# Which beats of the coupling take the score-maximum units: units by twos and fours alone

## The reference, cut to what matters

```python
x = x + layernorm(attn(layernorm(x)))     # 16 heads of width 8 on the left 128 columns
x = x + layernorm(ffn(layernorm(x)))

def attn(x):
    q, k, v = (left @ W.T for W in (Wq, Wk, Wv))          # per head
    att = softmax(einsum('qhd,khd->qkh', q, k) / 4, axis=k)
    return einsum('qkh,khd->qhd', att, v) @ Wo.T + bo

def ffn(x):                                # 3 cycles
    gf = global_net(x.mean(rows))
    for _ in range(3):
        tf = sigmoid(w4(gelu(w3(gelu(w2(gelu(w1(x))))))))
        coupling = 0.1 + ar * (0.7 * gf + 0.3 * tf - 0.5) * 2
        x = x + coupling * twist(x)
```

## Time and profile before

| | |
|---|---|
| median of 3 runs | 3399.24 us |
| span of the profiled execution | 3391.6 us |
| median less span | 7.6 us |
| PE busy | 3222.9 us (95%) |
| DVE busy | 2992.7 us (88%) |
| ACT busy | 2843.6 us (84%) |
| POOL busy | 897.6 us (26%) |
| mean granted TensorE clock | 0.985 |
| chain that ended last | PE 67%, DVE 17%, ACT 8%, issue 3%, SP queue 2% |
| unit's reduction, DVE line 966 (ring banks) | x3744, 683 ns each |
| unit's matmul, PE line 481 (ring banks) | x3744, 384 ns each |

### The profile page before, as it was taken

How to read it: one execution, slowest core, us unless ns; L and a number is a source line. 1 busy time by engine, 2 the same in 40 slices (tenths; PEclk the granted TensorE clock), 3 DMA queues, 4 the chain that set the end, 5 groups by cost and what they waited for, 6 DMA issues and landing times.

```text
span 3391.6 us, 56526 instructions
## 1 busy us (share of the span) xinstructions
PE 3222.9 (95%) x19712; PEld 941.5 (28%) x19712; DVE 2992.7 (88%) x5577; ACT 2843.6 (84%) x3752; POOL 897.6 (26%) x1322
## 2 busy tenths in 40 slices
PE   6989999999999999999999999999999999999987
PEld 2222232322323232232322323232232322323223
DVE  7999989999898998989989898998989989898943
ACT  3868979798897979979798897979979798896975
POOL 5002050321505123050320505123050320504015
PEclk7998999999999999999999999999999999999999
DMA  3111111121111112121121111112121121111001
GB/s 90 26 41 43 32 50 33 44 50 44 50 31 51 43 39 55 33 61 32 44 49 44 50 31 51 42 39 55 33 61 32 45 49 44 38 32 51 8 22 38
DMA packets 97498, 144.75 MB, mean 43 GB/s; under 512 B 49472, under 2 KB 60096, under 8 KB 89408
## 3 DMA queue, kind: packets, MB, share of 16 engines
q1 hardware_dynamic: 93520, 123.83, 13.8%
q0 software_dynamic: 3696, 17.31, 2.8%
HBM read 34.61 MB, written 32.51 MB: 20 GB/s over the span
## 4 chain that ended last, share of the span: by engine, by line
PE 67%; DVE 17%; ACT 8%; issue 3%; SPq 2%; DMA 1%; POOL 1%; DVEq 0%; POOLq 0%; ACTq 0%
PE heads_ps L514 24%; PE ring_ps L481 15%; DVE max_parts L966 12%; PE scoresT_ps L499 11%; PE scoresT_ps L602 7%; ACT p_sb L719 4%; DVE stats L977 3%; PE scoresT_ps L607 2%; ACT headsT L728 1%; PE ring_ps L543 1%; SPq L346 1%; DVE state L1030 1%; ACT state L784 1%; DVE moments L987 1%; PE ring_ps L529 1%
## 5 line engine op out<-in xcount | busy, mean ns | idle before, releaser
L966 DVE TENSOR_REDUCE max_parts<-ring_ps 128x1 f32<-128x512 f32 x3744 | 2369.2, 683 | 225.4 <-PE ring_ps L481 166.3
L719 ACT ACTIVATE p_sb<-scoresT_ps 128x1024 f32<-128x1024 f32 x2048 | 1970.1, 1024 | 81.4 <-PE scoresT_ps L499 57.7
L481 PE MATMUL ring_ps<-k_rows,q_rows 48*128 48x512 bf16 x3744 | 1086.0, 384 | 33.1 <-DVE max_parts L966 23.8
L514 PE MATMUL heads_ps<-p_sb,v_sb 128*9 128x512 f32 x8192 | 1071.4, 595 | 17.9 <-ACT headsT L728 11.9
L499 PE MATMUL scoresT_ps<-q_rows,k_rows 51*128 51x512 bf16 x4096 | 1021.3, 383 | 7.1 <-ACT p_sb L719 4.3
L481 PEld LDWEIGHTS ring_ps<-k_rows,q_rows 48*128 48x128 bf16 x3744 | 265.5, 94 | 1353.4 <-DVE max_parts L966 1242.4
L1233 POOL CAST max_wide<-max_all 128x16 bf16<-128x16 f32 x128 | 25.4, 198 | 1743.0 <-DVE max_all L972 1743.0
L602 PE MATMUL scoresT_ps<-state,w 128*128 128x512 f32 x732 | 364.9, 621 | 13.3 <-DVE state L1030 12.3
L824 ACT ACTIVATE p_sb<-scoresT_ps,b 128x512 f32<-128x512 f32 x180 | 123.8, 688 | 194.2 <-PE scoresT_ps L602 193.2
L499 PEld LDWEIGHTS scoresT_ps<-q_rows,k_rows 51*128 51x128 bf16 x4096 | 207.0, 93 | 224.4 <-ACT p_sb L719 211.5
L514 PEld LDWEIGHTS heads_ps<-p_sb,v_sb 128*9 128x9 f32 x8192 | 124.4, 88 | 288.8 <-issue 278.3
(11 more groups left out here) (196 smaller groups left out, 2635.9 us busy)
## 6 DMA issues: line engine op xcount, KB each, us to landing
q_rows<-parts SPq DMA_DIRECT2D x744, 32.0 KB
k_rows<-parts SPq DMA_DIRECT2D x744, 32.0 KB
x_sb<-in_x SPq DMA_DIRECT2D x16, 1024.0 KB, 4.8
x_in<-in_x SPq DMA_DIRECT2D x15, 1024.0 KB, 5.4
out<-x_sb SPq DMA_DIRECT2D x15, 1024.0 KB, 3.9
out<-x_in POOLq DMA_DIRECT2D x15, 1024.0 KB, 7.9
q_rows<-max_rows SPq DMA_DIRECT2D x512, 3.0 KB
feat_h<-headsT SPq DMA_DIRECT2D x512, 16.0 KB
```

Of the source, the lines that this page charges most:

```text
L481: e.matmul(ring_bank(max_taken, u + 1), q_rows[rows, slot, pair, h * BANK + qb * P:h * BANK + (qb + 1) * P], k_rows[rows, slot, pair, kh * ...
L514: m = e.matmul(heads_ps[32 * j:32 * j + DH + 1, :], v_sb[:, b % 2, kb, 4 * (group % NG) + j, 0:DH + 1], p_sb[:, n % 2, j, :], start=(kb == ...
L719: e.activation(p_sb[:, n % 2, 2 * two:2 * two + 2, :].rearrange("p h n -> p (h n)"), scoresT_ps[:, (2 - 2 * two) * BANK:(4 - 2 * two) * BA ...
L966: e.tensor_reduce(max_parts[:, gi % 2, kh, col:col + 1], bank_of(max_taken, u + 1), AX.X, ALU.max).then_inc(max_taken, 1)
```

## The change

The table of units per beat gets other numbers:

```diff
-BEAT_UNITS = (4, 1, 2, 1, 2, 1, 2, 2, 1, 1,
-              2, 3, 2, 3, 3, 2, 2, 4, 2, 1,
-              2, 1, 2, 3, 4, 2, 2, 2, 3, 1)
+BEAT_UNITS = (4, 0, 2, 2, 0, 2, 2, 2, 0, 2,
+              2, 2, 4, 2, 2, 4, 2, 4, 2, 0,
+              2, 2, 2, 4, 2, 4, 2, 2, 2, 2)
 IN_COUPLING = sum(BEAT_UNITS)
 IN_ATTENTION = UNITS - IN_COUPLING
```

## The result

The changed kernel takes 3413.24 us (median of 20 runs, 3408.47 to 3421.04) against 3398.90 for the kernel before (20 runs), a ratio of 1.0043 [1.0036, 1.0049]. It is slower by 0.4%. The forecast was 3397.7 with a range of 3382 to 3410, so the result lies above the range.

What follows compares the result with a forecast made beforehand. DVE was taken to bound beats 6 to 17, PE beats 20 to 27, ACT the end. Per coupling - 0.44 + 0.53 - 0.20 = - 0.11 us, times 14 - 1.5, giving 3397.7 us, range 3382 to 3410.

Steps and rivals of the forecast that it cites:

- The end.: Last beats of a coupling: 3 and 1 units become 2 and 2, ACT bounds, so 0 change.
- beats 0 to 5: Coupling's start to the first projection: the divide gates it, and it begins 0.44 us sooner on the mean.
- the other 1.2 us of PE's 1.60: Before the first projection: of 1.60 us PE is spared, 1.2 becomes waiting for the divide.
- Beats 6 to 17: Last y to update of beat 17: DVE bounds it, one unit more, sum + 0.53 us a coupling.
- the wait of 0.47: DVE's one wait in beats 6 to 17, into which the join of the maxima, moved to beat 9, would fit.
- the + 0.12 at beat 12: Beat 12: four units follow at once on the layer, where DVE was found 0.12 us early; a cost of 0.12.
- Beats 20 to 27: Layer of beat 20 to that of beat 27: PE bounds it, regrouped units take 2.66 for 2.85 us, - 0.20.
- fours at 0.72: Beats 20 to 27: alternative in which both groups of four units cost PE 0.72 us each, giving + 0.19.
- The constant of 7.6 us: Whole kernel: profiled execution's span lies 7.6 us below the median, carried along from 3390.1 to 3397.7 us.
- Rival 1: Whole coupling: PE's time counts in full, 2.66 us off each time, 37 us in all, 3362; chance 0.04.
- rival 2: At the projection: the divide is not the gate, PE's whole 1.60 us is gained, - 17.8 in all, 3381; chance 0.18.
- Rival 3: Beats 12 to 17: groups of four starve DVE, 0.8 us slower a coupling, 11 in all, 3410; chance 0.17.

Runs made afterwards that it cites:

- the last six beats alone: Old table of units per beat to beat 23, new one from beat 24, against the kernel before: 3405.55 us, 1.0026.
- the filler: Changed kernel with the score matmuls of attention's first step issued again over themselves: 3400.41 us, 1.0011 against the kernel before.
- the control: Kernel before with the same repeated score matmuls at attention's start, its table left alone: 3398.81 us, 1.0004.

## Why the prediction was wrong

- **The step that failed** is "*The end.* 3 and 1 units become 2 and 2; ACT bounds: 0", with its like in beats 0 to 5, "the other 1.2 us of PE's 1.60 turn into waiting for the divide". Both count PE's idle time as free. It is free on the critical path. But pairs side by side and longer waits left PE less busy, the granted clock fell to half, and the matmuls behind the wait, which are on the path, ran at 1.2 GHz: 1.6 us at attention's start in 4 of 14 stages, 1.6 and 2.9 at two late projections, 10.9 us in the trace, of the 15.5 that the two traces are apart (14.3 between the medians). Shown by the last six beats alone (+ 8 us at an unchanged coupling), by the filler (- 12.8 us), and by the control.
- **Beats 0 to 5: the mechanism right, the mean partly luck.** The reciprocal waits for the heads, 1.37 after their issue, the divide is at + 5.31, the projection 0.74 behind it. The mean gain at the projection is 0.48 us where 0.44 was forecast. But the forecast took SP's issue times over from the kernel before, stage by stage, and they came out otherwise: single stages gain from - 1.1 to 1.4 us where - 0.50 to 1.08 was forecast, and the waits of PE reach 2.8 us where 1.2 was. Only their mean stayed. The extra unit ahead of the divide costs its half microsecond where the heads come late, and 0.2 where they come early, as moving it showed.
- **Beats 6 to 17: the bound right, the sum partly luck.** + 0.59 where + 0.53 was forecast, and with fewer units the stretch shrinks, so DVE bounds it. Term by term: the extra unit cost its 0.60, and the update of beat 7 came 0.21 sooner for 0.19. But the join did not vanish in the wait of 0.47: it took 0.96 us beside POOL and made + 0.43 where nothing was put. Against that, the update of beat 10 takes 0.92 us instead of 1.15, - 0.24, which the forecast hasn't, and the + 0.12 at beat 12 is not there.
- **Beats 20 to 27: wrong in sign**, + 0.14 (16.96 for 16.82) where - 0.20 was forecast, 4.8 us in all between the two, and near the + 0.19 that the forecast gave for fours at 0.72. The four of beat 23 did cost 0.53, and the pair in place of the old four of beat 24 gave 0.40. But behind the four of beat 23 a Q or K projection started 0.15 later, for want of a bank; the four of beat 25 cost 0.22 more than the old pair of that beat, which had taken only 0.23 of the 0.32 I gave it; and in beat 26 the second unit waited 0.22 for a bank. I had counted banks in beats 12 to 17 and not here.
- Together the arithmetic of a coupling makes about + 0.25 us, some 3.5 us for the kernel (2.7 in the trace, with the first and last couplings shorter), within what the forecast called no difference. The clock makes most of the rest.
- **The constant of 7.6 us** between median and span is none. In every execution of the two kernels the time is 1.8 or 1.9 us above the span; the other 5.8 are what the traced execution is shorter than the median one. The forecast is not hurt by it, as the same 7.6 were taken off and put on.
- **The rivals.** Rival 1 and rival 2 are out: PE's 1.0 us less of busy time in a coupling did not shorten it, and DVE waited for the heads. Rival 3 named the right side and nearly the right size (3410), for a reason that the trace refutes: DVE had no wait in beats 12 to 17. That is luck.

Open: why the clock falls after the sixth, tenth, eleventh and thirteenth coupling and not after the others, whose PE timelines look alike at that place; and why SP issues the heads' DMAs up to 2.3 us later in some couplings than in others. With the new table and its banks in order PE is still idle for longer than before (5.29 us busy for 5.43), which fits the falls that stay and was not tested by itself. A fall at the projection is seen with the new front alone (none in the traces with the old front, where PE waits for the divide for 0.8 us at most, even with the reciprocal 9 us behind the first layer), but PE's wait there was not changed by itself.

## What to carry to other kernels

Before an engine's wait is booked at zero because another engine hides it, ask whether TensorE is the one that waits, and look at the granted clock just behind it: work taken off a busy TensorE can cost more than it gives. When a small reordering moves the time by more than its arithmetic, compare the granted clock by window before anything else, and ask how the traced execution's time lies to the median. And a gain on the engine that bounds a stretch is only had if the tables, banks and waits behind it are read again, since the rotation moves with every entry.

## What the runs showed of the hardware

- The granted clock of TensorE went to half in the middle of a kernel that keeps it 95% busy, after idle times of 0.57 and 0.40 us within one microsecond or two, or of 1.7 to 2.8 us in one piece. It did not after each of them, but after four of twelve attention starts that are alike, and two of four waits of 1.8 to 2.8 us in the changed kernel. Each such fall cost 1.6 to 2.9 us. I had looked at the clock of the kernel before, seen 1.00, and taken it as given.
- Ten score matmuls issued where four are needed, once a batch, took 12.8 us off the changed kernel and left the kernel before where it was (ratio 0.9995 to 1.0013).
- A DVE sum of two SBUF tiles took 1.30 us beside a sum on POOL, and 0.68 alone. The join of two tiles of 128x16 took 0.96 beside a product on POOL, and 0.18 alone.
- Data of the four DMAs of the heads were used 1.37 us after their issue had ended, in nearly all couplings; what made them late was the place in SP's queue.
- The same program ran with different mean clocks from one execution to the next: spans of 3406.7 to 3419.2 us at 0.981 to 0.978 for the changed kernel, 3391.2 to 3402.3 at 0.985 to 0.981 for the one before.
- Two units on the two row halves of the array start at the same time (both at 1921.29) and take 0.39 us together, so grouping by pairs lowers PE's busy time without shortening what surrounds it.
